# A delta-rule transformer block on one core: the head of the program in another order (x loaded first, norm rounds interleaved, the first projection beside the decays)

## The reference, cut to what matters

```python
xn = _layernorm(x, axis=-1)
# first attention: a gated delta rule over 8 heads
beta = sigmoid(xn @ Wb) * 2.0
g = -exp(A_log) * softplus(xn @ Wa + dt_bias); alpha = exp(g)
q = silu(causal_conv4(xn @ Wq)); k = ...; v = ...     # q, k then scaled to length 1
state = alpha * (state - beta * (state k) k^T) + beta * v k^T   # one step per token
out = rms(state q) * o_norm_w * silu(xn @ Wg)         # then @ Wo
# first feed-forward: a second norm of xn, then trees that route tokens to leaves
xf = (xn - mean(xn)) / sqrt(std(xn, ddof=1) + 1e-05)
```

## Time and profile before

| | |
|---|---|
| median of three runs | 3959.13 us |
| the profiled execution | 3963.87 us |
| its span, first to last instruction | 3961.9 us |
| TensorE busy | 83% of the span |
| VectorE busy | 55% |
| ScalarE busy | 35% |
| GpSimd busy | 25% |
| mean granted clock of TensorE | 0.876 of 2.4 GHz |

### The profile page before, as it was taken

The page is one execution under the profiler, slowest core; times in us unless marked ns, Lnnn a source line. Parts: engine busy times, 40 slices in busy tenths (PEclk is TensorE's granted clock), DMA queues, the critical chain, the costliest instruction groups (busy, mean ns, idle before and its releaser), DMA issues.

```text
span 3961.9 us, 87191 instructions
## 1 busy us (share of the span) xinstructions
PE 3295.1 (83%) x35570; PEld 2313.3 (58%) x35582; DVE 2183.2 (55%) x4825; ACT 1389.5 (35%) x3193; POOL 978.2 (25%) x988
## 2 busy tenths in 40 slices
PE   3478988788998788888768779656689999999998
PEld 3256666666766566666657657545355555545554
DVE  4457677366578466677246535514335454455444
ACT  1354444244444343344124422113333333433331
POOL 0012221412222412222317733346101101110110
PEclk6699998699798799898579989879789999999989
DMA  4201211301111301111248652473311111010000
GB/s 146 104 19 61 61 40 34 112 29 56 48 48 45 102 22 57 55 50 52 70 158 211 130 132 96 148 255 121 121 33 33 33 43 33 22 49 22 16 17 16
DMA packets 225224, 287.08 MB, mean 72 GB/s; under 512 B 34880, under 2 KB 171840, under 8 KB 224448
## 3 DMA queue, kind: packets, MB, share of 16 engines
q1 hardware_dynamic: 188608, 222.63, 17.4%
q0 software_dynamic: 27648, 50.49, 5.4%
q10 hardware_dynamic: 8576, 8.39, 0.6%
HBM read 187.72 MB, written 93.72 MB: 71 GB/s over the span
## 4 chain that ended last, share of the span: by engine, by line
PE 63%; DVE 15%; issue 6%; ACT 5%; DMA 4%; POOL 2%; another core or an unknown queue 1%; SPq 0%; DVEq 0%; POOLq 0%; ACTq 0%
PE banks L531 5%; PE banks L2878 5%; DVE s_d_kq L624 3%; PE banks L2450 3%; PE banks L767 3%; PE banks L2692 2%; PE banks L2434 2%; PE banks L1225 2%; PE banks L755 2%; PE banks L2462 2%; PE banks L1835 2%; PE banks L927 2%; PE banks L2602 2%; PE banks L925 2%; PE banks L1844 2%
## 5 line engine op out<-in xcount | busy, mean ns | idle before, releaser
L531 PE MATMUL banks<-s_d_xT,s_w_qkvg 128*128 128x512 f32 x640 | 348.5, 672 | 30.6 <-DMA s_d_xT<-xnT 21.2
L624 DVE SCALAR_TENSOR_TENSOR s_d_kq<-banks,s_conv_w,s_d_kq 128x511 f32<-128x511 f32 (+2 forms) x384 | 285.6, 745 | 51.9 <-ACT s_d_kq L576 37.8
L2564 ACT ACTIVATE s_g_pT<-banks 128x1536 f32<-128x1536 f32 (+1 forms) x96 | 153.0, 1594 | 436.1 <-PE banks L2452 436.1
L2528 DVE TENSOR_REDUCE s_g_nmax<-banks 128x4 f32<-128x512 f32 (+3 forms) x128 | 187.9, 1489 | 174.6 <-PE banks L2436 174.6
L1835 PE MATMUL banks<-s_q_xsT,s_q_w 128*128 x1008 | 169.3, 293 | 91.2 <-POOL s_q_w L1788 39.0
L2878 PE MATMUL banks<-s_m_we,s_m_tT 128*128 128x512 f32 x512 | 233.9, 602 | 3.5 <-DVE s_m_x L2941 3.2
L1835 PEld LDWEIGHTS banks<-s_q_xsT,s_q_w 128*128 128x128 f32 x1008 | 155.9, 202 | 128.1 <-issue 117.2
L531 PEld LDWEIGHTS banks<-s_d_xT,s_w_qkvg 128*128 128x128 f32 x640 | 128.1, 212 | 135.1 <-issue 112.9
L767 PE MATMUL banks<-s_d_TB,s_d_XT 32*32 32x32 f32 x9216 | 148.5, 203 | 67.0 <-issue 36.6
L2819 POOL TENSOR_TENSOR s_l_ex<-s_l_qk 128x512 f32<-128x512 f32 x32 | 33.3, 1041 | 662.3 <-DVE s_l_qk L2717 662.3
L767 PEld LDWEIGHTS banks<-s_d_TB,s_d_XT 32*32 32x32 f32 x9216 | 122.2, 114 | 126.9 <-issue 82.7
(11 more groups left out here) (391 smaller groups left out, 7653.2 us busy)
## 6 DMA issues: line engine op xcount, KB each, us to landing
s_q_w<-w12p SPq DMA_DIRECT2D x128, 257.0 KB
s_q_xs<-xs SPq DMA_DIRECT2D x32, 516.0 KB
s_d_E<-sums SPq DMA_DIRECT2D x64, 256.0 KB
s_r_xT<-xfT SPq DMA_DIRECT2D x12, 1024.0 KB
tree<-s_r_bias SPq DMA_DIRECT2D x96, 128.0 KB
s_r_work<-xf SPq DMA_DIRECT2D x24, 512.0 KB
og<-s_d_o SPq DMA_DIRECT2D x16, 512.0 KB
s_o_og<-og SPq DMA_DIRECT2D x16, 512.0 KB, 4.0
```

The lines of the kernel that those rows point to most:

```text
L531: ins = e.matmul(bk[6 + j % 2][:], w[:, par, c, self.COL[what] + h * P:self.COL[what] + (h + 1) * P], xT[:, c, :], start=(c == 0), stop=(c ...
L624: e.scalar_tensor_tensor(d[:, a:], bk[6 + j % 2][:, 0:SEQ - a], cw[:, par, k0 + 3 - a:k0 + 4 - a], d[:, a:], ALU.mult, ALU.add).then_inc(s ...
L2528: e.tensor_reduce(self.nmax[:, t, :].rearrange("p (k d) -> p k d", k=4)[:, :, 16], psum[:, 0:4, a:a + (t + 1) * P], AX.X, ALU.max, negate= ...
L2564: e.activation(self.pT[c][:], psum[:, 0:4, 0:self.COLUMNS[c]], ACT.Exp).then_inc(self.exped, 1)
```

## The change

- x of round 0 is issued by SyncE ahead of the constants. `Constants` is no stage of its own any more: its memsets stand at VectorE's start, its casts behind the first round's aggregates.
- `Norms`: a round is cut in two on VectorE. Its last part (`tail_vector`: the column and a/b copies) stands behind the statistics and aggregates of the next round. `step(i, n)` turns "instruction n of round i" into the count at its new place. SyncE issues x of round i+1 ahead of the stores of round i, and xnT of both sides ahead of xfT. TensorE no longer waits for VectorE's whole round.
- `Delta.load_weights` (3 MB and `conv_w`) is called by SyncE behind the constants, `load_columns` (xT of call 0) behind the stores of round 1.
- `Decays` is no stage of its own on four engines: its code is cut into 7 steps, and `walk` sets them beside the first 32 steps of project(e, 0) at a rate of 0.34. Behind these every engine waits for the decays to be over, then the other 18 steps follow.
- Tiles: `o` and `o2` are allocated ahead of the weights; `negm` and `negl` belong to `Norms`.

```diff
 class Norms:
     V, T, S = 29, 5, 5
+    HEAD, TAIL = 8, 3
...
+    def step(self, i, n):
+        if n > self.V - self.TAIL:
+            return self.V * (i + 1) + (self.HEAD + n - self.V if i + 1 < N_BATCH // 2 else n - self.V)
+        if i and n > self.HEAD:
+            return self.V * i + n
+        return self.V * i + n - (self.TAIL if i else 0)
...
     def sync(self, e):
-        e.wait_ge(self.g.over, 5 * self.n)
+        sides = [[self.sync_side(e, k, i) for k in range(2)] for i in range(N_BATCH // 2)]
+        for k in range(2):
+            next(sides[0][k])
+        self.constants.sync(e)
+        self.delta().load_weights(e)
         for i in range(N_BATCH // 2):
-            finish(self.sync_side(e, 0, i), self.sync_side(e, 1, i))
+            if i + 1 < N_BATCH // 2:
+                for k in range(2):
+                    next(sides[i + 1][k])
+            finish(*sides[i])
+            if i == 1:
+                e.wait_ge(self.cols_out[0], 64)
+                self.delta().load_columns(e)
...
     def vector(self, e):
-        e.wait_ge(self.g.over, 5 * self.n)
+        self.constants.small_vector(e)
         for i in range(N_BATCH // 2):
-            finish(self.vector_side(e, 0, i), self.vector_side(e, 1, i))
+            sides = [self.vector_side(e, k, i) for k in range(2)]
+            for _ in range(2):
+                for side in sides:
+                    next(side)
+            if i == 0:
+                self.constants.round_vector(e)
+            else:
+                finish(*(self.tail_vector(e, k, i - 1) for k in range(2)))
+            finish(*sides)
+        finish(*(self.tail_vector(e, k, N_BATCH // 2 - 1) for k in range(2)))
...
 class Delta:
+    OPEN = 32
...
     def walk(self, e, decays, project, invert, state, beside, first=None):
-        finish(project(e, 0))
+        opening = project(e, 0)
+        side_by_side((next(opening) for _ in range(self.OPEN)), (decays, 0.34))
+        finish(decays)
+        e.wait_ge(self.g.over, 5 * self.n)
+        finish(opening)
...
     def sync(self, e):
-        e.dma_start(self.w[:].rearrange("p a c n -> p a (c n)"), D["w_qkvg"].rearrange("a p c n -> p a (c n)")).then_inc(g.weights, 16)
...
+        self.decays.sync(e)
         self.decays_sync(e, 0)
-        self.walk(e, self.project_sync, self.invert_sync, self.state_sync, self.routes.steps_sync(e))
+        self.walk(e, iter(()), self.project_sync, self.invert_sync, self.state_sync, self.routes.steps_sync(e))
...
+    def load_weights(self, e):
+        D = self.g.dram
+        e.wait_ge(self.g.weights, Constants.END)
+        e.dma_start(self.w[:].rearrange("p a c n -> p a (c n)"), D["w_qkvg"].rearrange("a p c n -> p a (c n)")).then_inc(self.g.weights, 16)
```

More of the change, by code:

```diff
@@ L126, in sync, with small_vector, round_vector @@
             e.dma_start(t[:], D[n][None, :].broadcast_to((P, D[n].shape[0]))).then_inc(self.g.weights, 16)
-        e.wait_ge(self.g.weights, self.END)
-        e.sem_inc(g.over, 1)
-    def vector(self, e):
+    def small_vector(self, e):
+        g = self.g
+        e.memset(g.eps5[:], 1e-5).then_inc(self.rounded, 1)
+        e.memset(g.eps6[:], 1e-6).then_inc(self.rounded, 1)
+        e.memset(g.one[:], 1.0).then_inc(self.rounded, 1)
+    def round_vector(self, e):
         g = self.g
@@ L277, in scalar @@
     def scalar(self, e):
-        e.wait_ge(self.g.over, 5 * self.n)
+        e.wait_ge(self.constants.rounded, 3)
         for i in range(N_BATCH // 2):
@@ L293, in tensor_side @@
         yield
-        e.wait_ge(self.on_vector[k], v + 26)
+        e.wait_ge(self.on_vector[k], self.step(i, 26))
         for c in range(KC):
@@ L418, in tensor, with steps_gpsimd @@
         e.sem_inc(g.over, 1)
-    def gpsimd(self, e):
+        for _ in range(3):
+            yield
+    def steps_gpsimd(self, e):
         e.wait_ge(self.g.over, 5 * self.n)
         e.sem_inc(self.g.over, 1)
+        for _ in range(self.STEPS):
+            yield
 class Delta:
@@ L442, with __init__ @@
     STEPS, ITEM, GATE, VALUE, TURN = 50, 2, 22, 26, 30
-    def __init__(self, g, routes):
-        self.g = g
+    OPEN = 32
+    def __init__(self, g, routes, decays):
+        self.g, self.decays = g, decays
         self.n = g.stage()
@@ L1045, in invert_sync, with walk @@
             yield
-    def walk(self, e, project, invert, state, beside, first=None):
-        finish(project(e, 0))
+    def walk(self, e, decays, project, invert, state, beside, first=None):
+        opening = project(e, 0)
[3 more added lines that the diff above has]
+        finish(opening)
         if first is not None:
@@ L1089, in vector @@
     def vector(self, e):
-        e.wait_ge(self.g.over, 5 * self.n)
+        e.wait_ge(self.g.over, 5 * self.decays.n)
         e.wait_ge(self.g.weights, self.END)
-        self.walk(e, self.project_vector, self.invert_vector, self.state_vector, self.routes.steps_vector(e))
+        self.walk(e, self.decays.steps_vector(e), self.project_vector, self.invert_vector, self.state_vector, self.routes.steps_vector(e))
         e.wait_ge(self.o_normed, 4 * self.CALLS)
@@ L1097, in scalar @@
     def scalar(self, e):
-        e.wait_ge(self.g.over, 5 * self.n)
+        e.wait_ge(self.g.over, 5 * self.decays.n)
         e.wait_ge(self.g.weights, self.END)
-        self.walk(e, self.project_scalar, self.invert_scalar, self.state_scalar, self.routes.steps_scalar(e), self.decays_scalar)
+        self.walk(e, self.decays.steps_scalar(e), self.project_scalar, self.invert_scalar, self.state_scalar, self.routes.steps_scalar(e), self.decays_scalar)
         e.wait_ge(self.o_root, self.CALLS)
@@ L1104, in gpsimd @@
     def gpsimd(self, e):
-        e.wait_ge(self.g.over, 5 * self.n)
-        self.walk(e, self.project_gpsimd, self.invert_gpsimd, self.state_gpsimd, self.routes.steps_gpsimd(e), self.decays_gpsimd)
+        self.walk(e, self.decays.steps_gpsimd(e), self.project_gpsimd, self.invert_gpsimd, self.state_gpsimd, self.routes.steps_gpsimd(e), self.decays_gpsimd)
         e.wait_ge(self.o_gated, self.CALLS)
@@ L3052, in build @@
         g = Kernel(nc, ctx, dram)
-        stages = [Constants(g), Norms(g), Decays(g)]
-        delta = Delta(g, lambda: Routes(g, (0, 1, 2), "xf", "xfT", (5,)))
+        constants = Constants(g)
+        norms = Norms(g, constants, lambda: delta)
+        decays = Decays(g)
+        delta = Delta(g, lambda: Routes(g, (0, 1, 2), "xf", "xfT", (5,)), decays)
         segments = Segments(g, (0, 1, 2), ACT.Relu, delta.routes)
         attention = Attention(g, delta.routes)
-        stages += [delta, segments, attention, Seats(g, attention.routes)]
+        stages = [norms, delta, segments, attention, Seats(g, attention.routes)]
         stages += [Segments(g, (3,), ACT.Gelu, delta.routes, segments), SecondLayer(g)]
```

103 lines of the change are left out of this document (53 added, 50 removed).

## The result

The changed kernel took 3894.46 us in the median of four runs (3875.59 to 3913.55); before stood at 3958.24 (four runs). The ratio is 0.985, 95% interval 0.981 to 0.989: some 60 us less. The forecast was 3904, range 3890 to 3922. The profiled execution of the changed kernel is its fastest, 3875.59 us. Two more sets of the same kernel, of six runs each on other chips, gave 0.986 (0.983 to 0.989) and 0.985 (0.980 to 0.990).

What follows compares the result with a forecast made beforehand. TensorE bounds 63% of the whole span, but the changed first 145 us or so run through loads, VectorE and activation tables. Start 7.5, rounds 22.8 and opening 24.9 sum to 55.2 us off 3959.13: 3904 us, range 3890 to 3922.

Steps and rivals of the forecast that it cites:

- The start: Kernel start up to first xn: x issued first, xn at 14.7 instead of 22.66; 8.0 us, taken as 7.5.
- The rounds: Norm rounds, first to last xf: 79.5 us before, 56.0 after; 23.5 us gained, taken as 22.8.
- the 0.7 of round 2: Norm round 2: SyncE's column load ahead of x of round 3 costs 0 to 1.5 us, taken as 0.7.
- the wait for x behind the weights: First norm transition: 3 MB of weights delay the second x; without that cost, 1.5 us less.
- Rival 1: Norm rounds run at the high clock, 9.9 instead of 12.5, three times: 7.8 us less, 3896; chance 0.12.
- Rival 2: Norm rounds wait for transfers: 3913 if stores delay x, 3927 if none of x is hidden; chance 0.12.
- The opening: Read of ab to first kdec, with loads already there and decays beside the projection: 24.9 us gained.
- kinds that land late: End of the opening: kdec waits for the kinds' load; bounds 0 and 3 us, taken as 1.5.
- Rival 3: Opening runs cold: TensorE idles before item 4, then six items at 1.2 GHz cost 9 us, 3913; chance 0.12.
- Sum: Whole kernel: 7.5 + 22.8 + 24.9 = 55.2 us, subtracted from the median 3959.13 to give 3904 us.
- Rival 4: Slower: all that follows the head, shifted by 55 us, could be granted a lower TensorE clock; chance 0.02.
- my own sign: Trace from kdec on must be the old one shifted, else the forecast is wrong altogether; 5 us either way allowed.

Runs made afterwards that it cites:

- e8: Changed kernel with the first x issued behind the 15 constants, without waiting for them to land; 3889.1 us in one execution.
- e10: The changed kernel unedited, measured a third time; median 3888.1 us of six runs, ratio 0.985 to before.
- e1: The changed kernel unedited, measured a second time; median 3896.2 us of six runs, ratio 0.986 to before.
- e2: Changed kernel with only the norms part: weights and column block loaded behind the decays, decays whole ahead of the projection; ratio 0.9915 to before.
- e4: Changed kernel with the 3 MB of weights issued behind x of round 1 instead of ahead of it; ratio 0.985 to before.
- e5: Changed kernel with early loads kept but no projection steps beside the decays, which stand whole ahead of it; ratio 0.989 to before.
- e6: e4 with the exponential of A_log moved next to the first exponential, so three table loads instead of four; ratio 0.9875 to before.
- e7: e6 with VectorE's a/b copies moved behind the next round's reciprocals and xn; ratio 0.982 to before.
- e9: e7 with the 3 MB of weights issued one round later, behind x of round 2; ratio 0.988 to before.

## Why the prediction was right, point by point

- **The start** (8.0, taken as 7.5): 22.66 to 14.27, 8.4, and 8.3 to 8.7 in the other profiles of kernels that issue x first. x's 1 MB cost the constants nothing; the last landed at 13.2, forecast 13.5. Right. What e8 adds is the cause: of this gain 6.2 us are the place of x, and behind the constants x would also have come 3 us later after its issue.
- **The rounds** (first xf to last 56.7 at the low clock, the 0.7 of round 2 among it): e10, the one profile of the changed kernel with all three rounds at the low clock, shows 56.5. The sum was right, its first part not. I let the wait for x behind the weights set the first transition and made it 17.6; but at the low clock the a/b projections end later than that, and it is 18.9, as each of the others (18.6 to 19.0 against 19.2). The 0.7 for the column load in round 2 did not show. Forecast xf at 21.4, 39.0, 58.2 and 77.4 (78.1 with the 0.7); found 20.97, 38.55, 57.56 and 73.36. The 38.55 agrees by luck: that transition ran at the high clock, where x's wait does set it. The wait was 2.0 us where I had priced it at 1.5.
- **Rival 1, the high clock**, is not a case by itself, as I set it up, but a draw for each transition. In the changed profile the first and the third had it, in e1 the second, in e10 none; in all eight profiles with this order of the norms (e2, e4, e5, e6 and e8 too) it is 9 of 24 transitions, where I had given it 0.12. I had priced the high clock at 2.6 us a round; against 18.9 a round of 15.8 is 3.1. A row of windows (columns as in the earlier trace rows) shows it beside the idle stretch of the opening:

```profile
58.00:66.00 8.00, 7.00 (x48) 7.01 (x48) 7.90 (x28) 1.92 (x5) 0.00 (x0) 0.79 0.77 280
96.00:100.00 4.00, 1.92 (x4) 0.62 (x4) 0.00 (x0) 3.94 (x6) 0.00 (x0) 1.00 0.00 0
100.00:104.00 4.00, 1.28 (x2) 0.76 (x3) 3.51 (x7) 3.33 (x5) 0.00 (x0) 0.53 0.00 0
```

In the first row TensorE is busy 7.0 of 8 us and granted 0.79. The same pattern of instructions in round 1 of before got 0.50 at 10.3 of 12. The Trainium skill (TensorE: Matmul & The Clock Gate, Part 1) has it that activity releases the throttle; the rows agree that it can, but in 15 of the 24 transitions it didn't, so the rule alone does not forecast this stage.
- **Rival 2, rounds that wait for transfers**: not in the changed kernel, where the statistics of rounds 2 and 3 (41.14 and 60.15) start without a wait for x. It came up in e7 and e9, behind the a/b wait that they take away.
- **The opening** (ab to kdec 46.4): 46.67, 49.21 and 49.40. Taps were to end 38.5 us behind the read of ab and ended 38.7 behind it. Behind them I had 6.3 for the gate and the turning, and 1.5 for kinds that land late. Found were 8.0, but by another cause: the kinds don't stand in the chain; the gate's projection at the low clock does, 3.23 us at 126.97 where the old one took 1.99. The 1.5 us was right in size by luck, and wrong in what it named.
- **Rival 3, the cold opening**, was partly there in every run. In the last row above the clock falls from 1.00 to 0.53 behind TensorE's idle stretch, and item 4 takes 3.78 us (102.72) against 1.98. Without its 1.5 for the kinds my forecast is 44.9, and the three profiles lie 1.8 to 4.5 above that; so much at most the low clock costs in the opening, the gate's projection included, and not 9. Behind item 4 VectorE idles 1.25 us, where it idled 0.6 to 0.7 between items before: it has the decays' operations to do meanwhile.
- **Sum.** 55.2 us forecast; at kdec 60.1, 57.2 and 53.8 in the three profiles, mean 57.0; in time 64, 54 and 68 us between the medians of the three sets. e10 is the profile that meets the forecast's own terms, all rounds at the low clock: up to the first xf 8.5 (forecast 7.5), in the rounds 23.0 (22.8), in the opening 21.9 (24.9), and 0.4 in the tail of the last round, which I took as unchanged. The start was a little too small and the opening 3 us too large, and part of that cancels.
- **Rival 4, the clock of what follows**, exists as scatter; an effect of the change is not shown. Windows from kdec to the end, one row each, of before, the changed kernel, e5 and e7, all with the same instructions there:

```profile
194.00:3962.00 3768.00, 3212.55 (x35236) 2248.90 (x35248) 2093.36 (x4538) 1348.07 (x3102) 975.66 (x983) 0.89 0.23 70
```

```profile
134.00:3874.00 3740.00, 3193.42 (x35248) 2227.49 (x35248) 2095.93 (x4538) 1347.23 (x3101) 976.15 (x983) 0.89 0.23 70
```

```profile
146.00:3879.00 3733.00, 3181.48 (x35236) 2218.02 (x35248) 2096.35 (x4538) 1347.62 (x3103) 976.33 (x983) 0.90 0.23 70
```

```profile
129.00:3914.00 3785.00, 3235.80 (x35236) 2268.37 (x35248) 2096.47 (x4538) 1348.62 (x3103) 973.77 (x983) 0.88 0.23 70
```

VectorE is busy 2093 to 2096 us in all four. TensorE is busy 3181 (e5), 3193 (changed), 3213 (before) and 3236 us (e7), and the stretch lasts 3733, 3740, 3768 and 3785: 54 us more of TensorE, 52 us more of time. The changed kernel's own three profiles cover 3740 to 3753. The mean granted clock goes with it, 0.90 to 0.88. Single executions of before lie between 3923 and 3984. By my own sign the rest should have been the old one shifted, and I had given it 5 us either way: it lies 35 under to 18 above the 3768 of the one profile of before. That term was far too small, and that the median fell 10 us from the forecast is in part luck. The 28 us of the first pair are inside this scatter. The ratios of the three sets are gains of 55 to 60 us, beside 57.0 at kdec, but each is known only to 12 to 20 us, so an effect of the shift of some 10 us on what follows isn't excluded. What decides the draw wasn't tried.

## What to carry to other kernels

A head of serial loads and small stages is worth reading instruction by instruction: the mark at its end (here the first kdec) was forecast to 5 us, can be read to 0.1 in one profile and came within 6.3 us in three, while the time of the whole scatters by tens. Judge such a change by those marks and use the times to see that nothing was given back. When a wait is taken away, look for what is just under it: the weights' 2 us lay under the a/b copies at one clock and not at the other, and a 3 MB load that is put elsewhere can hold another round.

## What the runs showed of the hardware that I had not expected

- The same transfer of x took 4.2 us to its first use with nothing ahead, and 7.2 behind 15 small constants of 0.6 MB in all.
- Issuing one store of 512 KB takes SyncE 0.4 to 1.3 us in the norms of before and up to 2.1 in e2. With the 3 MB issued ahead, the longest took 3.1 us in e4, 3.9 in e7 (at 23.79) and 4.1 in e9.
- The granted clock of one and the same short stage (the a/b projections of a round) is 0.50 in one execution and 0.88 to 0.96 in the next, with the same instructions: 6.85 us or 3.7 to 4.1, and rounds of 15.8 or 19.0 us.
